# Matmuls of zeros at the seams of TensorE's stream, or one pass cut in two

## What is computed

```python
def _L0(x, adj, W, b):                       # batches left out
    num_neighbours = adj.sum(axis=-1, keepdims=True)
    return (adj @ (x @ W + b)) / num_neighbours

def _L1(x, adj, W1, b1, W2, b2, W3, b3):
    x = relu(adj @ (x @ W1) + b1)
    x = relu(adj @ (x @ W2) + b2)
    return adj @ (x @ W3) + b3

x = _layernorm(x + _L0(x, adj, L0_W, L0_b))
x = _layernorm(x + _L1(x, adj, L1_W1, ...))
```

## Time and profile before

| what | us |
|---|---|
| median of three runs | 551.56 |
| lowest and highest of them | 550.57, 553.27 |
| the profiled execution's own time | 553.69 |
| its span, first to last instruction | 551.9 |
| TensorE matmuls busy (3696) | 537.5 (97%) |
| TensorE weight loads busy (3696) | 496.1 (90%) |
| VectorE, ScalarE, GpSimd busy | 349.3, 307.4, 207.6 |
| mean granted TensorE clock | 0.996 |

### The profile page before, as it was taken

One profiled execution on the slowest core, in us unless ns is written; L12 is line 12 of the kernel. 1 busy time (PEld: TensorE's weight loads), 2 busy tenths in 40 slices (PEclk: granted clock), 3 DMA queues, 4 the chain that ended last, 5 costly groups with the idle time before them and its releaser, 6 DMA issues.

```text
span 551.9 us, 10683 instructions
## 1 busy us (share of the span) xinstructions
PE 537.5 (97%) x3696; PEld 496.1 (90%) x3696; DVE 349.3 (63%) x1034; ACT 307.4 (56%) x757; POOL 207.6 (38%) x223
## 2 busy tenths in 40 slices
PE   7799999999999999999999999999999999999996
PEld 6678998989899898998989899898999989899885
DVE  5675674756657475674756657475665757657455
ACT  4456546566555656655566554756655566553632
POOL 1654509053170714509063270814508062261000
PEclk9999999999999999999999999999999999999999
DMA  7730070521607034070512507043070612500002
GB/s 238 245 146 2 1 268 1 183 86 43 224 0 259 7 99 167 0 266 0 192 74 57 209 0 266 0 126 140 9 257 0 220 47 64 203 2 39 1 1 77
DMA packets 15287, 58.23 MB, mean 106 GB/s; under 512 B 1953, under 2 KB 2721, under 8 KB 13473
## 3 DMA queue, kind: packets, MB, share of 16 engines
q1 hardware_dynamic: 15264, 57.94, 29.2%
HBM read 49.55 MB, written 8.39 MB: 105 GB/s over the span
## 4 chain that ended last, share of the span: by engine, by line
PE 93%; DVE 3%; DMA 2%; ACT 1%; issue 0%; SPq 0%; DVEq 0%
PE bank_a L167 16%; PE bank_a L169 16%; PE bank_a L168 16%; PE bank_b L167 15%; PE bank_b L168 15%; PE bank_b L169 15%; DMA xT_raw<-in_xT 2%; DVE xT_lo L606 0%; DVE x_lo L606 0%; DVE v L655 0%; DVE x L662 0%; DVE stats L666 0%; DVE h_lo L606 0%; ACT x_hi L510 0%; ACT xT_hi L434 0%
## 5 line engine op out<-in xcount | busy, mean ns | idle before, releaser
L807 POOL TENSOR_TENSOR adj_lo<-adj_raw,adj_hi 128x512 fp32r<-128x512 f32 x56 | 70.8, 1296 | 269.2 <-ACT adj_hi L434 269.2
L606 DVE TENSOR_TENSOR x_lo<-bank_a,x_hi 128x512 fp32r<-128x512 f32 x64 | 44.3, 692 | 68.8 <-ACT bank_a L512 68.8
L167 PE MATMUL bank_b<-h_hi,adj_hi 128*128 128x256 f32 (+1 forms) x256 | 71.6, 280 | 3.3 <-DVE h_lo L606 2.6
L167 PE MATMUL bank_b<-s_hi,adj_hi 128*128 128x256 f32 x256 | 70.9, 277 | 0.9 <-DVE s_lo L606 0.9
L487 ACT ACTIVATE std<-moments,eps_col 128x1 f32<-128x1 f32 x64 | 18.9, 295 | 94.6 <-DVE moments L674 94.6
L169 PE MATMUL bank_b<-h_hi,adj_lo 128*128 128x256 f32 (+1 forms) x256 | 71.3, 279 | 0.0
L168 PE MATMUL bank_b<-h_lo,adj_hi 128*128 128x256 f32 (+1 forms) x256 | 71.3, 279 | 0.0
L169 PE MATMUL bank_b<-s_hi,adj_lo 128*128 128x256 f32 x256 | 70.9, 277 | 0.0
L168 PE MATMUL bank_b<-s_lo,adj_hi 128*128 128x256 f32 x256 | 70.8, 277 | 0.0
L510 ACT ACTIVATE x_hi<-bank_a,b_col 128x512 fp32r<-128x512 f32 x64 | 43.8, 684 | 21.6 <-PE bank_a L169 20.4
L794 POOL TENSOR_TENSOR x1b<-x,b_all 128x256 f32<-128x256 f32 x64 | 46.3, 759 | 17.2 <-DVE x L662 17.2
(11 more groups left out here) (97 smaller groups left out, 1608.5 us busy)
## 6 DMA issues: line engine op xcount, KB each, us to landing
adj_raw<-in_adjT SPq DMA_DIRECT2D x30, 512.0 KB, 5.4
adj_rows<-in_adj SPq DMA_DIRECT2D x14, 1024.0 KB, 9.4
x_raw<-in_x SPq DMA_DIRECT2D x16, 512.0 KB, 7.4
xT_raw<-in_xT SPq DMA_DIRECT2D x15, 512.0 KB, 6.6
out_y<-y SPq DMA_DIRECT2D x15, 512.0 KB, 2.9
w_raw<-in_w SPq DMA_DIRECT2D x4, 256.0 KB, 5.8
adj_rows<-in_adjT SPq DMA_DIRECT2D x2, 512.0 KB, 8.4
xT_raw<-in_xT SPq DMA_DIRECT2D x2, 256.0 KB, 4.4
```

The costliest lines, as they stand in the source:

```text
L167: pe.matmul(acc, st[0], mv[0], start=start, stop=False)
L606: return dve.tensor_tensor(lo, full, hi.bitcast(F32), ALU.subtract)
L807: pool.tensor_tensor(adj_lo[:, s, k, :], raw[:, k, :], adj_hi[:, s, k, :].bitcast(F32), ALU.subtract).then_inc(adj_split, 1)
```

## The change

`seam` and its two calls are removed. Instead `three_passes` takes a `cut`; where it isn't zero, the second pass is issued as two matmuls on the same stationary tile, the first over columns 0 to cut of the moving operand and of the sum, the second over the rest. `xw_product` hands the cut on for j = 0 and k = 0 alone. p6 gives 64, and p0 gives 64 where it has a reader and 0 for the second batch. p4 gives none. The waits are the same ones, now ahead of the first real matmul. Nothing else differs.

```diff
-        def three_passes(pe, acc, st, mv, start, stop):
+        def three_passes(pe, acc, st, mv, start, stop, cut=0):
 
             pe.matmul(acc, st[0], mv[0], start=start, stop=False)
-            pe.matmul(acc, st[0], mv[1], start=False, stop=False)
+
+            if cut:
+                pe.matmul(acc[:, 0:cut], st[0], mv[1][:, 0:cut], start=False, stop=False)
+            pe.matmul(acc[:, cut:], st[0], mv[1][:, cut:], start=False, stop=False)
             return pe.matmul(acc, st[1], mv[0], start=False, stop=stop)
...
-            def xw_product(done, bank, st, n, ready):
+            def xw_product(done, bank, st, n, ready, cut=0):
...
                         mm = three_passes(pe, bank[j][:, 0:F], (st[0](k, j), st[1](k, j)),
-                                          (w_hi[:, n, k, :], w_lo[:, n, k, :]), k == 0, k == KF - 1)
+                                          (w_hi[:, n, k, :], w_lo[:, n, k, :]), k == 0, k == KF - 1,
+                                          cut if j == 0 and k == 0 else 0)
...
-            def seam(bank):
-
-                pe.matmul(bank[:, 0:SEAM], zeros[:, 0:P], zeros[:, 0:SEAM], start=True, stop=True)
...
                         pe.wait_ge(reader, at(read, T, j + 1))
-                        if j == 0:
-                            seam(banks[0])
-
-                xw_product(p0_done, banks, (lambda k, j: xT_hi[:, j, k, :], lambda k, j: xT_lo[:, j, k, :]), 0, ready)
+
+                xw_product(p0_done, banks, (lambda k, j: xT_hi[:, j, k, :], lambda k, j: xT_lo[:, j, k, :]), 0, ready,
+                           0 if reader is None else SEAM)
...
                     pe.wait_ge(reader, at(read, T, j + 1))
-                    if j == 0:
-                        seam(bank_b[0])
 
                 pe.wait_ge(x3_split, at(old, KF, KF))
-                xw_product(p6_done, bank_b, (columns(x3_hi), columns(x3_lo)), 3, ready)
+                xw_product(p6_done, bank_b, (columns(x3_hi), columns(x3_lo)), 3, ready, SEAM)
```

## The result

The changed kernel takes 556.88 us in the median (555.68 to 558.77), the kernel before, measured beside it, 552.41 (550.57 to 553.69). The ratio is 1.0087 with a 95% interval of 1.0059 to 1.0115: slower by 0.9%, where 551.3 us had been forecast and the range ended at 554.8. The profiled execution took 558.77 us, its span is 557.0.

The account below looks back on a forecast made before the run. TensorE's matmul stream was taken to bound the kernel. Swapping zeros for the cut saves 0.01 us at each of 30 places, so 551.56 - 0.3 = 551.3 us, range 549.6 to 554.8.

Parts of the forecast that it names:

- What bounds the kernel: In the loop: TensorE, busy in 97% of the span, waits for nothing; its matmul stream sets the step's period.
- points (1) to (3): At p6 and p0: zeros go, second matmul becomes two with one load more; -0.01 us per place, -0.3 us over 30.
- Point (4): After p0's zeros, matmuls come 0.12 us apart for a while, costing 0.02 to 0.03 us; assumed to stay.
- the unrest that had been priced as a bound: At p6: if it caught the same wider matmul spacing as p0, 16 x 0.03 = 0.5 us more.
- The first rival: Stream falls out of step: p0, p4 and p1 at 0.118 us per matmul after the cut, 557.5 us, chance 0.17.
- the sum itself: At each cut, first real matmul to third pass: 0.33 to 0.35 us against 0.35 with zeros.
- The other rivals: At the cut: no second load, 547.4 us, chance 0.05; shorter load, 549.5, 0.03; narrow pieces dearer, 553.1, 0.01.

## Why the prediction was wrong

**What bounds the kernel: right.** TensorE waits for nothing within the loop in the changed kernel either; all that its phases gained in length is in the span. The distance of two steps, which was to shrink by 0.00 to 0.04 us, grew by 0.40.

**The exchange, points (1) to (3): right in mechanism and size.** Loads and matmuls are 3696 each, the second piece has its own load, the two stalls add up to one load, and four instructions take 0.46 instead of 0.47 us. Forecast was 0 to 0.02 us less. One detail came out otherwise: the third pass starts 0.32 us after the first real matmul (99.34 to 99.66), sooner than the 0.33 to 0.35 of the sum, and gives it back by lasting 0.14 instead of 0.113 to the next start.

**Point (4), the unrest behind p0's zeros: wrong.** It was assumed to stay as it was, 0.02 to 0.03 us. In its place came the slow pace for all of p0: 2.93 instead of 2.87 us. At p6 the unrest that had been priced as a bound (0.5 us in all) came in part: 0.02 us per step, 16 x 0.02 = 0.3 us.

**The first rival was what happened, and it had 0.17.** Its price was nearly right. It named p0, p4 and p1, 96 matmuls at 0.118 us, 14 times, +6.2 us. Measured were 14 x 0.40 = 5.6, as p0 had carried part of that loss before the change already. Its time, 557.5, lies 0.6 us above the median measured, and that is in part luck: the two medians measured side by side differ by 4.5 us, and that of the kernel before was 0.9 above the 551.56 from which the forecast set out. The step that failed is the sum itself, which put the pace of the matmuls behind the cut at no change, and the sentence on which that rests: the cut makes the same kind of stall, a matmul in the queue without weights, even twice. In place of no change, p4 and p1 took 0.32 us more per step and p0 0.06. The sentence took any stall for a cure. The runs showed that a stall decides nothing by its kind: 64 and 192 columns fail in the second pass and work in the first, 32, 128 and 192 work where 64 and 96 fail, and with the tiles 64 bytes further on even the zeros fail. With a cure of unknown mechanism in the kernel, its form couldn't be taken to be free, and the range should have reached over 557.5 us. The evidence was in the rows: p4 of the last batch and the last p7 at 0.118 us were read as a pace that keeps itself up, and then given a small chance.

**The other rivals** are out. The load isn't dropped, it isn't shorter than 0.11 us, and the narrow pieces cost no more than their columns.

**What stays open.** That the slow pace depends on where the tiles lie, and that it is carried from phase to phase, is shown. That it comes from two reads that meet in the same part of the memory would fit both, and is only argued. The trace of the kernel before narrows down what could meet. In its last p7, at the slow pace, there is a stretch of six matmuls in 0.70 us in which no other engine and no DMA works (us, then PE, PEld, DVE, ACT and POOL busy, granted clock, DMA share, GB/s):

```profile
541.86:542.56 0.70, 0.70 (x8) 0.70 (x7) 0.00 (x0) 0.00 (x0) 0.00 (x0) 1.00 0.00 0
```

So nothing outside TensorE is needed to keep the slow pace up; whether something outside can start it is open, and so is what within TensorE holds each matmul back by 0.005 us. Nor does any run explain why the five widths come out as they do.

The Trainium skill (TensorE: Matmul & The Clock Gate, Step-by-step: what each phase is for) says of a load beside a matmul: "Loading the next tile's weights doesn't steal SBUF read bandwidth from the running matmul." By this rule, moving the tiles would change nothing between these two; the step went from 32.97 to 33.87 us with 64 bytes. If the slow pace doesn't come from those two reads, the rule may still stand.

## What to carry to other kernels

Where a stream of matmuls has columns that just cover its weight loads (here 0.113 us against 0.11), read the pace of every phase, not only the changed place: a difference of 0.005 us per matmul in phases left alone was most of the result (0.32 of 0.40 us per step). If such a kernel holds an odd-looking instruction, try the kernel without it, then forms that hide its cost under a wide neighbour, and take no other form of it on trust. Before such tuning, fix where the tiles lie: a pad of 64 bytes moved the kernel before by 0.90 us per step, the edit by 0.40.

## What was not expected of the hardware

- The same instructions with the same operands ran at two stable paces, 0.113 and 0.118 us per matmul of 256 columns, at a granted clock of 1.00, and kept a pace over up to 96 matmuls and three phases. With the tiles 64 bytes further on, p4 had a third, 0.120. The slow pace held while no other engine and no DMA worked.
- With no short matmul, the stream changed its pace twice a step, always at the same places: to slow where p6 begins, to quick where p0 begins.
- 64 bytes between two groups of tiles cost 0.90 us per step in the kernel before (33.87 against 32.97) and 0.39 in the changed one (33.76 against 33.37); there 512 and 1024 bytes left the step as it was.
- A cut of a 512-column matmul into 280 and 232 is nearly free: 0.23 us for both.
